# Four-layer graph network: node work of the attention and relation layers put into their edge loops, in units of four tiles

## What is computed

```python
edge_index = jnp.stack([src, dst])
x = _layernorm(x + attention0(x))    # 4 heads of 32, softmax over the edges that enter a node
x = _layernorm(x + mlp(x))           # gelu(layernorm([x[src], edge_attr] @ W1)) @ W2, summed by dst, node update, + x
x = _layernorm(x + relation(x))      # x @ W[r] + bias[r], gated, gathered by (src, type), summed by dst, + x @ loop_weight, relu
x = _layernorm(x + attention3(x))    # as attention0, + bias, layernorm with gamma and beta, relu
```

## Time and profile before

| what | us |
|---|---|
| median of 3 runs (4850.43 to 4851.74) | 4851.01 |
| the profiled execution, its own time | 4856.42 |
| its span, first to last instruction | 4854.6 |
| PE, DVE, ACT, POOL busy | 3016.2, 2483.6, 1327.0, 3239.6 |
| the four stretches of gathers, first start to last end | 1040.1, 1041.7, 1039.7, 1039.8 |
| what lies before, between and behind them | 75.3, 112.4, 273.0, 95.2, 137.2 |

### The profile page before, as it was taken

How to read it: one execution, slowest core, us unless ns; L and a number is a source line. 1 busy time by engine, 2 the same in 40 slices (tenths; PEclk the granted TensorE clock), 3 DMA queues, 4 the chain that set the end, 5 groups by cost and what they waited for, 6 DMA issues and landing times. The chain is left out here.

```text
span 4854.6 us, 53090 instructions
## 1 busy us (share of the span) xinstructions
PE 3016.2 (62%) x15318; PEld 2692.3 (55%) x15318; DVE 2483.6 (51%) x4658; ACT 1327.0 (27%) x3623; POOL 3239.6 (67%) x3391
## 2 busy tenths in 40 slices
PE   3777677776677777777383333333345776777762
PEld 3666666664567677766343333333345666666661
DVE  3444444445799999997671111111134444444447
ACT  0000000002699999997450000000011000000003
POOL 4777777772677777775017777777746777777761
PEclk7665666656899999998695555555576666666665
DMA  4344444431444444442052222222214444444430
GB/s 130 109 109 109 109 110 112 109 105 45 133 119 119 119 119 119 119 119 85 14 214 53 53 53 53 53 53 53 53 29 122 109 109 109 109 109 111 111 82 27
DMA packets 249279, 458.28 MB, mean 94 GB/s; under 512 B 104966, under 2 KB 147208, under 8 KB 249000
## 3 DMA queue, kind: packets, MB, share of 16 engines
q0 software_dynamic: 119808, 280.51, 22.8%
q1 hardware_dynamic: 129192, 174.48, 11.0%
HBM read 411.70 MB, written 43.03 MB: 94 GB/s over the span
## 5 line engine op out<-in xcount | busy, mean ns | idle before, releaser
L783 POOL DMA_INDIRECT rows<-gat_table,src_i x1664 | 1573.3, 946 | 531.8 <-issue 531.8
L971 PE MATMUL p_adc<-adw,hot_t 128*128 128x8 f32 x3328 | 655.8, 335 | 558.2 <-DVE hot_t L809 558.0
L783 POOL DMA_INDIRECT rows<-rel_table,rel_i x832 | 786.4, 945 | 313.5 <-issue 247.8
L971 PEld LDWEIGHTS p_adc<-adw,hot_t 128*128 128x128 f32 x3328 | 638.4, 294 | 629.4 <-DVE hot_t L809 628.5
L783 POOL DMA_INDIRECT rows<-mlp_table,src_i x832 | 788.4, 948 | 264.7 <-issue 264.7
L1004 PE MATMUL p_sum<-hot,rows 128*128 128x128 f32 x1664 | 384.3, 425 | 669.8 <-issue 643.5
L991 PE MATMUL p_sum<-rows,hot 128*128 128x133 f32 x3328 | 759.1, 417 | 4.2 <-DVE rows L832 4.2
L1004 PEld LDWEIGHTS p_sum<-hot,rows 128*128 128x128 f32 x1664 | 359.3, 328 | 695.4 <-issue 695.4
L991 PEld LDWEIGHTS p_sum<-rows,hot 128*128 128x128 f32 x3328 | 714.7, 318 | 5.2 <-DVE rows L832 5.2
L998 PE MATMUL p_sum<-hot,rows 128*128 128x128 f32 x3328 | 458.1, 303 | 232.0 <-ACT rows L949 231.9
L998 PEld LDWEIGHTS p_sum<-hot,rows 128*128 128x128 f32 x3328 | 438.5, 216 | 272.8 <-ACT rows L949 272.8
(11 more groups left out here) (207 smaller groups left out, 3301.0 us busy)
## 6 DMA issues: line engine op xcount, KB each, us to landing
drow<-in_dst_rows SPq DMA_DIRECT2D x208, 512.0 KB
rows<-gat_table,src_i POOLq DMA_INDIRECT x1664
rel_table<-tab SPq DMA_DIRECT2D x49, 512.0 KB, 2.6
rows<-mlp_table,src_i POOLq DMA_INDIRECT x832
eat<-in_edge_t SPq DMA_DIRECT2D x104, 128.0 KB
rows<-rel_table,rel_i POOLq DMA_INDIRECT x832
gat_table<-tab SPq DMA_DIRECT2D x14, 479.5 KB, 4.7
mlp_table<-tab SPq DMA_DIRECT2D x7, 896.0 KB, 4.1
```

The lines of the kernel that those rows point to most:

```text
L783: pool.indirect_dma_start(out=rows[:, st.slot, t, :], out_offset=None, in_=table[:, :], in_offset=bass.IndirectOffsetOnAxis(ap=of[:, st.gr ...
L971: last = nc.tensor.matmul(p_adc[k][:, t, 0:2 * H], hot_t[:, k, t * P:(t + 1) * P], adw[:, half, :], start=True, stop=True)
```

## The change

The node work of both attention layers and of the relation layer moves into the edge loops; the phases `gat_finish`, `mlp_tables`, `rel_finish` and the second `gat_tables` are gone. Since the edges are sorted, a node's sums are final long before the pass ends. Units of 4 tiles are formed (11 of 4 tiles, then 3 and 2), and each gets a step of the loop, `at`, from which its pieces are spread over the following steps. For this input the steps are 9, 18, 26, 35, 43, 52, 60, 69, 77, 86, 94, 100 and 105. A new term of the `fits` flag checks that no later group reaches back into a finished unit.

- First attention pass: a unit's sums are turned straight from `net.acc`, divided, added, normalised, turned again, multiplied by W1 and stored as rows of the MLP's table. VectorE clears the unit's part of `net.acc` (GpSimd did so for the whole in `mlp_tables`).
- Relation pass: the same with the loop weight's product, then the rows of the last layer's table, `h_self` and `att`. The bound over all nodes and the store of `adc_table` come once, behind the loop.
- Last pass: both layer norms and the store of the output.
- `p_sum` and `p_turn` of the attention pass have one buffer now, which makes room in PSUM for `p_node` and `p_keep`; the last layer's gamma and beta are read from PSUM.
- The version for `fits` = 0 gathers once a group, not once a window. The MLP pass is written anew for that, with the same instructions in the fast version.
- The last unit's pieces lie behind the last group in every engine's program (its step is 105, at least 5 behind that of the unit before).

```diff
+UNIT = 4
+SLACK = 64
+APART = 5
+    for u, m in enumerate(sizes):
+        end = (first + m) * P
+        after = ng - 1 if end >= n else min(ng - 1, -(-(end + SLACK) * e // (n * GE)) - 1)
+        at = max(after, at + APART)
+        units.append(Unit(u, first, m, after, at))
...
+def drive(sh, stages, pieces):
+    most = max([lag for _, lag in stages] + [lag for _, lag in pieces] + [0])
+    for step in range(max(sh.NG, sh.units[-1].at + 1) + most):
+        for stage, lag in stages:
+            if 0 <= step - lag < sh.NG:
+                stage(step - lag)
+        run_units(sh, step, pieces)
...
+def gat_pass(net, layer):
+        p_sum = s.ps("p_sum", [P, 512])
+        p_turn = s.ps("p_turn", [P, 512])
+            def gather(n):
+                wait(pool, s.summed, n - RING + 1)
...
+            def divide(unit):
+                dve.wait_ge(s.node_sums, unit.u + 1)
+                if last:
+                    nc.vector.tensor_tensor(by_head(o[:, 0:m, :]), own, e[:, tiles, :].unsqueeze(3).broadcast_to([P, m, H, C]), ALU.mult)
...
+                nc.vector.reciprocal(share[:, 0:m, :], rd[:, 0:m, :])
+                nc.vector.tensor_tensor(by_head(pa[:, 0:m, :]), by_head(pa[:, 0:m, :]), share[:, 0:m, :].unsqueeze(3).broadcast_to([P, m, H, C]), ALU.mult)
...
+                    nc.vector.tensor_tensor(net.x[:, tiles, :], pa[:, 0:m, :], net.x[:, tiles, :], ALU.add)
+                    nc.vector.memset(net.acc[:, :, columns(unit)], 0.0)
+                    unit_moments(nc, six, net.x[:, tiles, :], m)
+                variances(nc, six, work, m)
+                dve.drain().then_inc(s.variance, 1)
...
+            pieces = [(divide, 4), (factors, 5)]
+            pieces += [(residual, 6), (outer_factors, 7)] if last else [(evacuate, 8)]
+                drive(sh, [(logits, 1), (one_hot, 0), (weigh, 1), (add, 2)], pieces)
...
+                pieces = [(root, 4), (inner_normalise, 5), (outer_root, 6), (normalise, 7)]
+                pieces = [(root, 4), (normalise, 5), (copy_x, 6)]
+                drive(sh, [(weights, 1), (copy_sums, 1)], pieces)
...
+            def add_up(n):
+                pe.wait_ge(s.messages, n + 1)
+                wait(pe, s.sums_copied, n)
+            def turn(n):
+                pe.wait_ge(s.sums_copied, n + 1)
+                wait(pe, s.added, n)
+            def turn_sums(unit, fast):
+                pe.wait_ge(s.added, all_added(unit, fast))
+                wait(pe, s.normed if last else s.tab_done, unit.u)
...
+                rest = [] if last else [(turn_x, 6), (multiply, 7)]
+                return [(lambda unit: turn_sums(unit, fast), 3)] + rest
+                drive(sh, [(turn, 2), (spread_adc, 0), (add_up, 1)], pieces(True))
...
+def rel_pass(net):
+            pieces = [(residual, 4), (factors, 5), (evacuate, 8)]
+            pieces = [(copy_x, 2), (root, 4), (normalise, 5), (copy_new, 6), (keep, 8)]
+                return [(turn_x, 2), (lambda unit: multiply(unit, fast), 3), (turn_new, 6), (tables, 7)]
...
-        edge_pass(net, "gat")
-        gat_finish(net, last=False)
-        mlp_tables(net)
-        edge_pass(net, "mlp")
+        gat_pass(net, 0)
+        mlp_pass(net)
         mlp_finish(net)
         rel_tables(net)
-        edge_pass(net, "rel")
-        rel_finish(net)
         net.h_self = ctx.enter_context(nc.sbuf_tensor("h_self", [P, sh.NT, F], F32))
-        gat_tables(net, 1, keep_self=True)
+        rel_pass(net)
         segment_max(net, keep_self=True)
-        edge_pass(net, "gat")
-        gat_finish(net, last=True)
+        gat_pass(net, 1)
```

More of the change, by code:

```diff
@@ L44 @@
 BIG = 3.0e38
-Shapes = namedtuple("Shapes", "N E NT NP NW NG NB NBATCH BN")
-Step = namedtuple("Step", "n slot visit group col base")
+Shapes = namedtuple("Shapes", "N E NT NP NW NG NB NBATCH BN units")
+Unit = namedtuple("Unit", "u first tiles after at")
 def shapes_of(n, e):
@@ L64, in wait @@
     eng.wait_ge(sem, value)
[L67 to L93, removed]
 def uses_before(i, k):
@@ L167, in phase @@
 @contextmanager
-def phase(net, names, rings=()):
+def phase(net, names, *rings):
     nc = net.nc
@@ L664, in pick @@
     with eng.If(fits == 1):
-        program(True)
+        fast()
     with eng.Else():
[L667 to L682, removed]
-    nc, sh, a = net.nc, net.sh, net.ins
[L685 to L691, removed]
+        slow()
@@ L710, in edge_pass @@
[L710 to L734, removed]
+        drow = s.sb("drow", [P, HALF, GE], I32)
@@ L736, in _, with all_added @@
+        ph = [p[:, :].rearrange("p (t c) -> p t c", c=HID) for p in p_node]
+        table = net.mlp_table.rearrange("(t p) c -> p t c", p=P)
+        out = net.out.rearrange("(t p) f -> p t f", p=P)
+        stored = [s.stored0, s.stored1]
+        LOADS = 3 if last else 2
+        def all_added(unit, fast):
+            return unit.after + 1 if fast else sh.NG * sh.NT
         @s.block.sync
         def _(sp):
[L738 to L764, removed]
-            pick(sp, net, lambda fast: drive(sp, sh, [(lambda st: load(st, fast), [0])], fast))
@@ L1230, in _, with add_up @@
-            pe.wait_ge(s.w_done, 1)
-            sweep(pe, sh, [(turn, 0), (multiply, 1)])
+            def add_up(n):
+                pe.wait_ge(s.onehot, n + 1)
+                pe.wait_ge(s.gathered[n % RING], (n // RING + 1) * 16 * T)
+                wait(pe, s.added, n - 1)
+                for t in range(T):
+                    end = nc.tensor.matmul(p_sum[n % 2][:, 0:P], rows[:, n % RING, t, :], hot[:, n % HALF, t, :], start=(t == 0), stop=(t == T - 1))
+                end.then_inc(s.summed, 1)
```

1273 lines of the change are left out of this document (806 added, 467 removed).

## The result

The changed kernel takes **4626.4 us** (median of 4 runs, 4624.9 to 4626.9) where the kernel before takes 4851.4 in the same group of runs: ratio 0.9535, 95% interval 0.9518 to 0.9551. The forecast was 4628. The profiled execution took 4624.9 us, its span is 4623.0.

What follows compares the result with a forecast made beforehand. GpSimd's gathers were taken to pace the passes, so only uncovered stretches could shrink: -75.6 - 55.2 - 93.6 + 0.7 + 1 = -222.7 from 4856.4 gives 4633.7, less the 5.4 offset 4628 us; range 4605 to 4665.

Steps and rivals of the forecast that it cites:

- The bound: All passes: GpSimd's (POOL's) gathers alone set the pace, 10.0 us per group of 8, 1040 us per pass.
- Gap 1: Between first attention pass and MLP pass: 112.4 us shrinks to 36.8, saving 75.6.
- Gap 2: Between relation pass and last attention pass: 95.2 us shrinks to 40.0, saving 55.2.
- The end: From the last gather to the span's end: 137.2 us shrinks to 43.6, saving 93.6.
- Start: Before the first gather: one more small load and a few one-row operations add 0.7 us.
- Passes: Gather loops with node work woven in: new work costs 0 on the path, gathers +1 us over three passes.
- The offset of 5.4: Whole kernel: the runs' median lies 5.4 us below the profiled execution, taken as the same after the change.
- A: Attention groups: single buffers make a serial chain, 14.2 us against 10.0 per group, time about 5500 us; 3%.
- C: Passes: unit work reaches the pace; 33 ScalarE table loads on the path cost 42 us, 4670 us; 4%.
- D: Gaps and end: last units start late or take twice the time, up to 4704 us; 8%.
- E: `fits` flag: its new term falls to 0, so every pass takes over 40 ms; under 1%.
- B: Last pass: VectorE operations with two SBUF inputs hold gathers through the port, 15.3 us, time 4643 us; 12%.

Runs made afterwards that it cites:

- e2: Changed kernel plus one VectorE product of two SBUF inputs (1024 columns) in each of the relation pass's 104 groups: 4674.1 us, ratio 0.9642.
- e1: Changed kernel with the first attention pass's 13 units run behind its loop instead of inside it: 4817.4 us, ratio 0.9936.
- v1b: Changed kernel with shorter lags between a unit's pieces, units 4 groups apart, last units of 2 then 3 tiles: 4602.2 us, ratio 0.9493.
- e6b: Changed kernel with GpSimd's counter increment put back in front of each group's gathers in the three passes: 4623.7 us, ratio 0.9537.
- e4: Kernel before the change, with single `p_sum` and `p_turn` buffers in both attention passes: 4849.0 us, ratio 1.0001.
- e5b: Changed kernel plus a square root on ScalarE in every group of the last pass, forcing table loads: 4632.1 us, ratio 0.9554.
- e3: Changed kernel plus one VectorE SBUF-to-SBUF copy of 1024 float32 columns in each of the relation pass's 104 groups: 4641.4 us, ratio 0.9573.
- v1: Same kernel as v1b, on a chip where the kernel before took 5729.3 us: 5406.3 us, ratio 0.9444.
- e5: Same kernel as e5b, on the chip where the kernel before took 5729.3 us: 5423.9 us, ratio 0.9473.
- e6: Same kernel as e6b, on the chip where the kernel before took 5729.3 us: 5538.3 us, ratio 0.9662.

## Why the prediction was right

**The bound.** "The passes are thus paced by POOL alone" held: 104 groups in 1038 to 1040 us in all four passes, with the node work inside. e2 shows it from the other side: what lengthens gathers lengthens the pass, us for us. e1 shows that covering is all there is to gain in gap 1, since the same units uncovered cost 194 us more there.

**Gap 1**, forecast 36.8, measured 37.2. The parts: 6.1 to the divide (6.1 forecast), 13.9 for the unit of 3 (12.6), 11.9 for the unit of 2 (11.5), 5.4 to the next gather (6.6).

**Gap 2**, forecast 40.0, measured 43.8. To the sums 6.6 (6.1), unit of 3 11.5 (10.1), unit of 2 8.7 (9.8, for TensorE begins it while the one before is finishing), and 17.0 where "14.0, unchanged" stood. That is the term that was mis-sized. The timeline shows where, first of the kernel before and then of the changed one:
```profile
3664.13 0.51 DVE L513 TENSOR_REDUCE most<-att 128x4 f32<-128x196 f32 x1
```
```profile
3529.35 0.18 DVE L1363 COPY att<-tab 128x16 f32<-128x16 f32 x1
3532.78 0.50 DVE L1396 TENSOR_REDUCE most<-att 128x4 f32<-128x196 f32 x1 [3.26 <-issue]
```
From this operation to the first gather both take 13.4 us (3664.13 to 3677.55, 3532.78 to 3546.20), so all 3.0 lie ahead of it. VectorE waits for nothing the trace names for 3.26 us, at the place where its program leaves the pass for the bound. I took the stretch over from before, where other code stood ahead of it. v1b has the same idle time (2.83 us), so it belongs to this place and not to one run; what it is, wasn't tried.

**The end**, forecast 43.6, measured 37.8. To the divide 6.2 (6.1), unit of 3 15.1 (16.5), unit of 2 13.2 (15.3), and 3.3 after the last normalising instead of 5.7. Two terms were too dear in the units. The factors' chain, for which I took 3.3 us from the chain over 49 tiles, takes 2.5 over 2 or 3 tiles (4602.76 to 4605.27 for one), in three of its four places here. And for handing over between engines I had 1.0 in each unit, where 0.03 to 0.07 us pass at each turn. The range carried it ("10 less").

**Start**, forecast +0.7, measured +1.5 in this execution; but the repeat of the same kernel began its gathers at 75.0, so nothing is left to explain.

**Passes**, forecast +1, measured -5.8. No experiment finds a part of the change that does this: e6b excludes the dropped increment, and the kernel before, with single buffers (e4), had a span of 4846.6 with gathers of 944 ns. The difference of the mean gathers, 946.0 against 944.3, times 3328 is 5.7 us, so it is the durations of the gathers, which differ from execution to execution. The offset of 5.4 between the profiled execution and the median of before is most likely the same thing; v1b's profiled execution, with gathers of 947 ns, lies 7 us above its median too.

**How much of the hit is luck.** I took that offset over as "the same", and so two errors cancelled: against the profiled execution's 4856.4 the sum gave 4633.7 and it was 4624.9, against the medians 4628 and 4626.4. Gap 2 (3.8 too short) and the end (5.8 too long) cancelled in part as well. The mechanism is borne out by the parts; the 2 us are luck. And the range's low end was not worked out from its own terms: these give 14 us less than the forecast (4.0 and 10), 4614, where I wrote 20 less and 4605.

**Rivals.** A (single buffers) is refuted by e4, and by the changed kernel's passes themselves. C is refuted by e5b. D did not occur: the gaps stayed under 50; e1's gap, 24 us above what I expected, shows that units of 4 in series are the ones I cost too low. E did not occur. B, to which I gave 12%, is right in kind and small in size. Of the 22 operations with two SBUF inputs that lie beside gathers in the last pass (L962 and L1002, 11 each), five, all of L962, lengthened a gather, by 0.7 us together; in the repeat of the same kernel six did, by 1.0, and in the other kernels of the first and third group up to 13, by up to 2.9. I had 15.3 for all of them holding throughout. My reading of the earlier trace rows was half of it: VectorE waits in some places, as e3's copies do, but I took from it that gathers don't, and that was wrong; no long operation of that kind had run beside gathers. The Trainium skill ("SBUF — State Buffer", section "Who interferes with whom") says that copies can contend with GpSimd, and operations with two SBUF inputs with a GpSimd instruction that reads SBUF, and that the one that issues first blocks the other throughout. It infers that a product of two tensors leaves descriptor generation alone. That copies contend, e3 shows too. The rest these runs do not bear out: e2's products held 96 gathers, a product that began inside a gather did not wait for it, and copies that began 0.18 to 0.5 us into a gather held it, though the gather was first.

## What to carry to other kernels

Where one engine's issue paces a loop, work of the others costs nothing inside it and its full length outside, unless it holds the pacing engine itself, as e2's products do (0.45 us each). So the first number to work out is what is left uncovered, and it is the last units' chain, not the work as a whole: 37 us of 112 here, and 29 once the unit before the last was done in time. Splitting alone was a loss: e1 was 119 us worse in its gap than the undivided work, so the units paid only because the gathers lay over them. And the lags, the distance and the order of the units are worth tuning even where the loop has room, because they decide how many units are still open at the end.

## What was not expected of the hardware

- A VectorE product of two SBUF inputs holds a gather that starts under it: the gather ends 0.81 us behind the product, if that is later than its own 0.94 us (e2). It holds a gather that has started before it not at all. A copy of 0.69 us can hold a gather that has already begun, or wait for it, by how far the gather is (e3). With gathers every 1.25 us, one operation of 1.23 us cost 0.45 us in the mean; the 22 operations of 0.69 us in the changed kernel cost 0.03 each in its profiled execution, for only five fell so. The 1024-column operations with one input in PSUM (L919, L913 and L945, 208 each) run beside the same gathers; in the whole first pass none but the very first gather took over 970 ns.
- The mean duration of an indirect gather differs between executions of one kernel: 944.0 ns in v1 and 947.0 in v1b, on two chips, of which some 2 ns are in every pass and the rest are held gathers. Over 3328 gathers 3 ns are 10 us, as much as the difference a measurement of this kernel can tell.
- The same kernel took 4849 us on one chip and 5729 on another. In the three kernels traced on the other one, gathers took the same 944 to 948 ns, but a group took 11.5 to 11.7 us in the mean in the attention and MLP passes of v1 and e5 (11.9 to 12.1 in e6) instead of 10.0, and in v1 VectorE worked 50 us and more behind the gathers over most of these passes. In v1's relation pass most groups took 10.0 us, and 29 of 103 took 10.6 to 23.6. The gain held its ratio there (v1: 0.9444, v1b: 0.9493 here); the kernel before was not traced on that chip, so why isn't shown.
